# Blur stage: GpSimd's subtraction of the means waits for the variance sums instead of the means

## The reference, cut to what matters

```
def _gn(v, G=32, eps=1e-05):
    B_, C_, H_, W_ = v.shape
    g = v.reshape(B_, G, C_ // G, H_, W_)
    m = jnp.mean(g, axis=(2, 3, 4), keepdims=True)
    s = jnp.var(g, axis=(2, 3, 4), keepdims=True)
    return ((g - m) / jnp.sqrt(s + eps)).reshape(v.shape)
...
x = x + _L0_conv_ref(_gn(x), L0_conv_sigma)
```

## Time and profile before

| | us |
|---|---|
| median of 3 runs | 3322.46 |
| lowest, highest | 3321.8, 3325.74 |
| the profiled execution | 3321.49 |
| its span | 3319.5 |
| PE busy | 2512.4 (76%) |
| DVE busy | 2113.5 (64%) |
| ACT busy | 1819.4 (55%) |
| POOL busy | 1148.1 (35%) |

### The profile page before, as it was taken

The page is one execution under the profiler, slowest core; times in us unless marked ns, Lnnn a source line. Parts: engine busy times, 40 slices in busy tenths (PEclk is TensorE's granted clock), DMA queues, the critical chain, the costliest instruction groups (busy, mean ns, idle before and its releaser), DMA issues. The chain is left out here.

```text
span 3319.5 us, 86457 instructions
## 1 busy us (share of the span) xinstructions
PE 2512.4 (76%) x38569; PEld 1493.1 (45%) x38569; DVE 2113.5 (64%) x2867; ACT 1819.4 (55%) x1855; POOL 1148.1 (35%) x788
## 2 busy tenths in 40 slices
PE   1774639184999953879999955579999095999998
PEld 0664213022777741235555532157776032555555
DVE  5997767763555546547777758355554663777775
ACT  1111737573555545647767747545555482766775
POOL 0221000101555522654454410055553174444442
PEclk7887879586999976979999977789999596999999
DMA  2455030501111144212222241201111712222221
GB/s 62 122 156 161 19 101 1 202 8 28 28 27 33 25 161 166 57 62 80 83 83 86 81 162 73 28 19 33 28 31 28 303 39 52 80 83 84 85 82 61
DMA packets 213122, 257.73 MB, mean 78 GB/s; under 512 B 79188, under 2 KB 141192, under 8 KB 210696
## 3 DMA queue, kind: packets, MB, share of 16 engines
q1 hardware_dynamic: 203528, 218.58, 22.5%
q0 software_dynamic: 9216, 33.56, 2.5%
HBM read 153.52 MB, written 98.57 MB: 76 GB/s over the span
## 5 line engine op out<-in xcount | busy, mean ns | idle before, releaser
L2053 PE MATMUL dense_spread<-dense_cp,kept_spread_yx 32*128 32x512 f32 x2432 | 479.1, 665 | 67.3 <-DVE dense_cp L2212 60.0
L1323 ACT ACTIVATE snake_samp<-snake_s 128x1024 f32<-128x1024 f32 x320 | 321.3, 1024 | 299.5 <-PE snake_s L1253 299.2
L2232 DVE TENSOR_TENSOR dense_hat<-dense_spread,dense_hat 128x1024 f32<-128x1024 f32 x256 | 301.6, 1220 | 246.7 <-PE dense_spread L2053 246.7
L1386 DVE TENSOR_SCALAR snake_hat<-snake_spread 128x1024 f32<-128x1024 f32 x256 | 301.5, 1219 | 205.1 <-PE snake_spread L1231 205.1
L2157 ACT ACTIVATE dense_hat<-dense_spread 128x1024 f32<-128x1024 f32 x256 | 248.8, 1023 | 284.1 <-PE dense_spread L2053 278.0
L1253 PE MATMUL snake_s<-snake_hat,snake_xt 64*64 64x128 f32 x10240 | 337.5, 274 | 19.4 <-ACT snake_samp L1323 19.1
L2177 ACT ACTIVATE dense_samp<-dense_s 128x864 f32<-128x864 f32 (+1 forms) x384 | 299.1, 833 | 78.6 <-PE dense_s L2103 78.5
L2103 PEld LDWEIGHTS dense_s<-dense_hat,dense_xt 64*64 64x64 f32 x11264 | 267.9, 134 | 145.4 <-issue 95.5
L1253 PEld LDWEIGHTS snake_s<-snake_hat,snake_xt 64*64 64x64 f32 x10240 | 284.9, 133 | 86.0 <-issue 42.2
L657 PE MATMUL dcnoff_acc<-dcnoff_low,kept_w_off 128*64 128x512 f32 x384 | 175.0, 611 | 181.9 <-DVE dcnoff_high L647 177.7
L2103 PE MATMUL dense_s<-dense_hat,dense_xt 64*64 64x108 f32 x11264 | 308.9, 257 | 0.5
(11 more groups left out here) (315 smaller groups left out, 4894.7 us busy)
## 6 DMA issues: line engine op xcount, KB each, us to landing
dense_cp<-offs SPq DMA_DIRECT2D x576, 56.0 KB
x<-blur_x SPq DMA_DIRECT2D x16, 1024.0 KB, 5.1
gateconv_xn<-x SPq DMA_DIRECT2D x16, 1024.0 KB, 11.0
pre<-snake_ob SPq DMA_DIRECT2D x32, 512.0 KB, 3.9
dense_xr<-x SPq DMA_DIRECT2D x64, 256.0 KB, 3.1
out<-dense_xr SPq DMA_DIRECT2D x64, 256.0 KB, 2.5
dense_cp<-offs SPq DMA_DIRECT2D x256, 48.0 KB
offs<-dcnoff_cm SPq DMA_DIRECT2D x64, 144.0 KB
```

Source lines behind the costliest of these rows:

```text
L1323: act.activation(samp[u % 2][:, :, i * MS:(i + 1) * MS, :, :].rearrange("p b m t h -> p b (m t h)"), sample_at(u, i)[:, :, :], ACT.Copy).t ...
L1386: ins = dve.tensor_scalar(strided(hat[u % 2][:, 0:1], GUARD + (4 * tau + 2 * half) * SW * SR, [[8, 2], [SW * SR, 2], [SR, SW], [1, 8]]), s ...
L2053: return pe.matmul(bank[:, :], k.spread_yx[r, kind, :], cp[u % 2][r, tile, :], start=True, stop=True)
L2232: dve.tensor_tensor(h, p_hat[pair][:, :, :].rearrange("p t (r x) -> p (t r) x", x=W), h, ALU.mult).then_inc(main_ready, 1)
```

## The change

The instruction that GpSimd runs for each chunk is the same. What it waits for is another semaphore: `spread_ready`, which DVE raises with L251, in place of `mean_kept`, which DVE raises with L242. Both count one per chunk. In DVE's list L251 stands three instructions behind L242.

```
             def centre(t, slot, before, last):
-                pool.wait_ge(mean_kept, t + 1)
+                pool.wait_ge(spread_ready, t + 1)
                 if before >= 2:
                     pool.wait_ge(half_ready, (t - 1) * Q)
```

## The result

The changed kernel takes 3274.47 us (median of 4 runs, 3274.11 to 3274.59) against 3323.3 us for the kernel before (4 runs: the 3 of the table and one more). The ratio is 0.9852, with a 95% interval of 0.9835 to 0.9869: 48.8 us less. Forecast were 3273 us and 48.8 us. The profiled execution has a span of 3272.4 us.

The account below looks back on a forecast made before the run. DVE was taken to bound the blur at 13.665 us per period. Gains of 46.9 + 2.1 less 0.2 give 48.8 us, from 3321.49 to 3272.7; with 1.0 for the median, 3273 us. Range of 8 in 10: 3268 to 3287.

Parts of the forecast that it names:

- The stall of L247: Blur, DVE: L247 falls from 3.524 to 0.175 us per period, 46.9 us over 14 periods.
- GpSimd's later start: Blur: GpSimd starts 0.98 us behind L242, putting the centred chunk 0.64 us later.
- L264 beside GpSimd: Blur, DVE: the sixteen L264 now run during GpSimd's subtraction; costed at nothing, like L2232.
- the other end: Blur, DVE: L264 stalls fully beside GpSimd like L2246, 3.3 us per chunk, eating the whole gain.
- Rival B: Blur, DVE: the stall moves to L264 through its per-partition scalar; 1.6 us longer, 3324 us; chance 0.06.
- The margin of TensorE's loop: Blur: the loop over GpSimd and PE closes in 9.98 us against DVE's 10.32, 0.34 us to spare.
- TensorE's clock: Blur, PE: full clock behind a 1.7 us gap; otherwise 0.98 us more per period for two slow groups.
- Rival A: Blur: PE becomes the bound through its clock or a slower GpSimd signal; gain 38.9 us, 3284 us; chance 0.17.
- The ends of the stage: Blur's first and last chunk: 0.2 us lost at the first, 2.1 us gained at the last.
- the stages behind the blur shift as a whole: Stages after the blur: they begin at a barrier and move with the blur's end.
- C: Blur: queued L264 shut GpSimd out until the last of sixteen is through; slower, 3343 us; chance 0.04.
- the transfers: Blur loads and stores, 1 MB each per period: hidden, with 20.6 us slack measure against 27.3 before.

Follow-up runs that it names:

- run 1: Kernel before, GpSimd's wait unmoved: difference written to both PSUM and SBUF, so square and sum each read one operand from PSUM; 3273.27 us, ratio 0.9856.
- run 2: As run 1, but the square is written to SBUF, so the sum reads two SBUF tensors; 3317.65 us, ratio 0.9988.
- run 3: Changed kernel with L264 reading x twice from SBUF, blurred result left out; 28909 us in all through another branch, blur period 13.75 us.
- run 5: As run 4, with ten more matmuls per chunk into an unused PSUM bank behind the last L315; 3280.25 us, ratio 0.9875.
- run 4: Changed kernel with GpSimd's wait moved one step further, to TensorE's variance matmul (var_ready); 3313.37 us, ratio 0.9977.
- run 7: Kernel before, GpSimd's wait unmoved: ScalarE squares the difference, TensorE averages squares and row variances by two matmuls; 3262.75 us, ratio 0.9825.
- run 6: Kernel before with eight more matmuls per chunk into an unused PSUM bank ahead of TensorE's wait for spread_ready; 3320.55 us, ratio 0.9999.

## Why the prediction was right

The gain agrees to 0.1 us, and that is luck. In the profiled executions the span is 47.1 us shorter, not 48.8: the blur gave 0.6 us more than forecast and the stages behind it took back 2.3. And the median of the kernel before was 3323.3 us beside the changed kernel, but 3321.2 to 3322.2 beside the nine others. What was right is the mechanism and the terms, as follows.

**The stall of L247** was the term that carried the sum: 46.9 us forecast, 46.88 measured. Its cause is shown by runs 1 and 2, which turn the stall off and move it without touching GpSimd's wait.

**GpSimd's later start**: 0.98 us behind L242 forecast, 0.96 measured, and its end to L306 took 0.14 us where I allowed 0.1.

**L264 beside GpSimd** cost nothing, as taken from L2232. Run 3 shows what the other end would have been, and that it hangs on the second SBUF tensor and not on the scalar. Rival B's price was worked out with a slip: today the sixteen end 166.01 + 4.23 - 161.89 = 8.35 us behind L242, not 8.50, so its own sum would have been a period of about 14.0 us. In run 3 they end 8.41 behind L242, and the period is 13.75.

**The margin of TensorE's loop** was set too thin, at 0.34 us; this is the term that the prediction had wrong in size. Run 5, where that loop is the bound, shows its true length: from L306 to L290 it takes 4.62 us (143.21 to 147.83) and not 5 x 0.97 = 4.85, and from L290 to L242 0.33 and not 0.43. With the start of the changed kernel that is 0.96 + 3.61 + 0.14 + 4.62 + 0.33 = 9.66 us, 0.66 to spare. The period of run 5 agrees: GpSimd starts 2.14 us behind the copy, 1.18 later, and 1.18 - 0.66 = 0.52 is what 10.84 has over 10.32.

**TensorE's clock** stayed at 1.00 as forecast. The outcome was right, the reason given only half so. I had argued from the length of a gap: 1.73 us left the clock alone, 2.4 us did not the earlier trace rows. Run 4 has gaps of 2.9 us behind which it fell and others behind which it held, so the length of one gap does not decide. Rival A did not occur: the gaps ahead of L306 were 1.58 to 1.76 us from the second chunk on, the clock held behind all of them, and DVE waited 0.49 us before L242. How far it was from occurring no run shows. But its price was too low: with GpSimd 1.2 us later the clock cost 33 us, not the 14 x 0.98 = 13.7 us of its working.

**The ends of the stage.** The first period was to cost 0.2 us and cost nothing (11.94 against 11.97). From the sixteenth L242 to the last L264 are now 13.32 us, 2.36 less, forecast 2.1. The blur thus ends 49.4 us earlier (251.22 against 300.66), 0.6 more than forecast, but the span is only 47.1 us shorter. Of the 2.3 us between, the gate convolution behind the blur takes 1.5, from its first load to that of the next stage (296.4 us before, 297.9 now). Its instructions are the same. Why it takes longer stays open; over the profiles of these kernels this stage lies between 295.1 and 297.9 us, which is also 2.6 of the 3.4 us that run 7 has less. The prediction's sentence that the stages behind the blur shift as a whole holds to these 2.3 us and no better. (It also put the blur at 230 us; from its start at 64.4 to its last L264 it is 236. Nothing hangs on that.)

Rivals B and C did not occur; the transfers stayed hidden at 0.69 DMA share.

## What to carry to other kernels

A tiny instruction with a long duration and no idle time ahead of it may be held inside the engine: compare it with its neighbours of the same shape, and with what GpSimd does in that time. Here it was enough that one operand of the VectorE instruction came from PSUM (run 1), or that the small two-operand steps were done before GpSimd was let loose; moving them to ScalarE and TensorE (run 7) was better still. Each such delay must be weighed against the loop that passes through GpSimd: here 0.6 us later was free, and 1.2 us more cost 39 us.

## What the runs showed of the hardware that was not expected

VectorE's sixteen queued instructions with two SBUF tensors did not keep GpSimd out: GpSimd started 0.23 us behind the first, ran its 3.61 us, and one of the sixteen took up to 3.75 us meanwhile (run 3). Two SBUF tensors cost VectorE a whole GpSimd instruction; with one SBUF tensor and the scalar from SBUF the longest of 256 took 0.35 us.

The granted clock after a pause of TensorE is not a matter of that pause alone. Behind pauses of 2.92 to 2.94 us in run 4 the two groups L306 took the 2.05 us of full clock three times, and 2.46 to 3.78 us five times; behind pauses of 2.76 us, which are shorter, they never took less than 2.79 us (seven times). And in run 6 it fell in the middle of dense work, at 162 us, over matmuls that ran from 160.65 without a pause, having had 2.3 us of idle time before them:

```profile
161.00:162.00 1.00, 1.00 (x11) 1.00 (x11) 0.85 (x3) 0.00 (x0) 0.58 (x1) 1.00 0.02 8
162.00:163.00 1.00, 1.00 (x8) 1.00 (x7) 1.00 (x1) 0.60 (x1) 1.00 (x1) 0.52 0.29 27
```

What decides it these runs do not show. Ten matmuls per chunk without use won 33 us (run 5 against 4).
